# Layer 1's row maxima formed as b + relu(a - b) by three engines, instead of one reduction over 1024 scores

## The reference, cut to what matters

```python
q = q_vec.reshape(B_H, S, QK_DIM)
k = k_vec.reshape(B_H, S, QK_DIM)
qn = jnp.sum(q * q, axis=-1)[:, :, None]
kn = jnp.sum(k * k, axis=-1)[:, None, :]
qk = jnp.einsum('bsd,btd->bst', q, k)
scores = -(qn + kn - 2.0 * qk) / tau
attn = jax.nn.softmax(scores, axis=-1)
out = jnp.einsum('bst,btc->bsc', attn, v)
```

## Time and profile before

| | |
|---|---|
| median of 3 runs | 8861.34 us (8860.65 to 8866.9) |
| span of the profiled execution, first to last instruction | 8833.4 us |
| mean granted TensorE clock in it | 0.889 |
| busy: PE / DVE / ACT / POOL | 84% / 64% / 44% / 25% |
| layers 1 to 3 | from about 3540 us to the end |

### The profile page before, as it was taken

One profiled execution on the slowest core, in us unless ns is written; L12 is line 12 of the kernel. 1 busy time (PEld: TensorE's weight loads), 2 busy tenths in 40 slices (PEclk: granted clock), 3 DMA queues, 4 the chain that ended last, 5 costly groups with the idle time before them and its releaser, 6 DMA issues.

```text
span 8833.4 us, 95654 instructions
## 1 busy us (share of the span) xinstructions
PE 7445.8 (84%) x35246; PEld 3495.5 (40%) x35246; DVE 5679.0 (64%) x9661; ACT 3844.7 (44%) x7430; POOL 2220.5 (25%) x1862
## 2 busy tenths in 40 slices
PE   7989889989989995668888888888888888888867
PEld 4544444445544452123333333333333333333343
DVE  4666656566665663457667667766766766766674
ACT  4444444444544552443543543444354354354330
POOL 1222222222222220012421421331231232133152
PEclk9999999999999996679899889899888888888988
DMA  1111111111111112024444544554444454354375
GB/s 64 35 38 37 36 37 38 40 38 44 42 42 38 41 38 72 4 78 118 153 141 107 169 150 112 149 163 116 133 152 129 117 160 144 97 167 146 99 220 145
DMA packets 244211, 849.75 MB, mean 96 GB/s; under 512 B 46413, under 2 KB 49177, under 8 KB 243361
## 3 DMA queue, kind: packets, MB, share of 16 engines
q1 hardware_dynamic: 150272, 388.71, 16.4%
q0 software_dynamic: 92160, 453.06, 16.2%
q10 hardware_dynamic: 1312, 1.87, 0.1%
HBM read 602.10 MB, written 89.68 MB: 78 GB/s over the span
## 4 chain that ended last, share of the span: by engine, by line
PE 39%; DVE 13%; ACT 6%; DMA 3%; issue 3%; SPq 2%; POOL 1%; DVEq 0%; ACTq 0%; POOLq 0%
PE ps L2189 10%; PE ps L2649 4%; PE ps L2434 4%; DVE arena L1901 4%; PE ps L2199 3%; PE ps L2660 2%; PE ps L2630 2%; PE ps L2127 2%; PE ps L2320 2%; SPq L2683 2%; PE ps L2113 2%; DMA arena<-arena 1%; DVE arena L400 1%; DMA arena<-img,arena 1%; PE ps L2152 1%
## 5 line engine op out<-in xcount | busy, mean ns | idle before, releaser
L2467 POOL DMA_INDIRECT arena<-img,arena x1152 | 1369.8, 1189 | 2685.6 <-DMA img<-arena 1859.8
L2364 DVE SCALAR_TENSOR_TENSOR arena<-arena 128x384 f32<-128x384 f32 x1152 | 748.0, 649 | 656.6 <-DMA arena<-img,arena 653.6
L1901 DVE TENSOR_REDUCE arena<-ps 128x2 f32<-128x1024 f32 x768 | 894.3, 1216 | 322.6 <-PE ps L2168 319.6
L2042 ACT ACTIVATE arena<-ps 128x512 f32<-128x512 f32 x1536 | 817.5, 603 | 315.1 <-PE ps L2199 312.4
L2189 PE MATMUL ps<-arena 128*64 128x512 f32 x3072 | 935.7, 711 | 0.0
L982 POOL TENSOR_TENSOR arena<-arena 128x512 f32<-128x512 f32 x384 | 442.1, 1158 | 1942.5 <-DMA arena<-decay 1942.4
L2649 PE MATMUL ps<-arena 128*64 128x512 f32 x3072 | 808.1, 651 | 129.6 <-DMA arena<-arena 73.9
L2434 PEld LDWEIGHTS ps<-arena 128*96 128x96 f32 x4608 | 557.9, 174 | 202.1 <-issue 201.7
L2434 PE MATMUL ps<-arena 128*96 128x128 f32 x4608 | 610.4, 289 | 26.3 <-DVE arena L2353 26.2
L1115 DVE TENSOR_TENSOR arena<-ps,arena 128x512 f32<-128x512 f32 x384 | 265.4, 691 | 492.3 <-issue 270.5
L949 PE MATMUL ps<-arena 128*128 128x512 f32 x1152 | 507.2, 596 | 0.0
(11 more groups left out here) (344 smaller groups left out, 12092.7 us busy)
## 6 DMA issues: line engine op xcount, KB each, us to landing
arena<-arena SPq DMA_DIRECT2D x1024, 144.5 KB, 2.9
arena<-decay SPq DMA_DIRECT2D x384, 256.0 KB, 3.2
img<-arena SPq DMA_DIRECT2D x162, 384.0 KB, 2.6
arena<-img,arena POOLq DMA_INDIRECT x1152, 4.5
arena<-y SPq DMA_DIRECT2D x16, 768.0 KB, 6.4
arena<-x SPq DMA_DIRECT2D x16, 768.0 KB, 6.3
out<-arena SPq DMA_DIRECT2D x16, 768.0 KB
arena<-x SPq DMA_DIRECT2D x16, 512.0 KB, 5.1
```

The lines of the kernel that those rows point to most:

```text
L1901: dve.tensor_reduce(out, self.wides[B.at("max", b, g, n, h) // 2].rearrange("p (a b) -> p a b", a=2), AX.X, AL.max).then_inc(*S.mark("max_ ...
L2042: act.activation(self.p[n % 6], B("score", b, n)[:, :], ACT.Exp).then_inc(*S.mark("p_act", b, n))
L2364: dve.scalar_tensor_tensor(gb[:, 0:384], gb[:, 384:768], pp[:, 1, n:n + 1], gb[:, 0:384], AL.mult, AL.add).then_inc(*S.mark("corner_x", b, n))
L2467: pool.indirect_dma_start(self.g[n % 6], None, img, bass.IndirectOffsetOnAxis(ap=ii[:, n:n + 1], axis=0)).then_inc(*S.landed(f"{self.tag}g ...
```

## The change

For each block of 128 query rows, a holds the scores of the first 512 keys and b those of the last 512. The largest of both is the largest element of b + relu(a - b). TensorE forms a - b in PSUM with two accumulated matmuls (the second one against `kn`, the negated second half of the keys, which VectorE writes once per g) and b with a third. ScalarE takes the relu of a - b from PSUM into an SBUF buffer of 512 columns (`self.p[m % 4]`, one of four). VectorE adds b to it and keeps the running maximum in one instruction, `tensor_tensor_reduce`, that also writes the sum back into the buffer. So a step has six matmuls, two relus and two `tensor_tensor_reduce` of 512 columns, in place of four matmuls and two reductions of 1024. Banks are now taken one by one from all five, in the order diff, diff, max, max for each step. In layer 3, ScalarE's gelu moves one step of the second stream earlier, so it now stands ahead of the relus of the step that it followed. The joining of the two halves at `mt` becomes a copy.

```diff
@@ Layer1.__init__
+        self.kn = ar([96, 2, 512], BF16)
@@ Layer1.dve, rows
+            if side:
+                dve.wait_ge(*S("split_dve", b, 1, g, 1))
+                dve.tensor_scalar(self.kn[:, g, :], ks[:, g, H(1)], -1.0, None, AL.mult).then_inc(*S.mark("less_k", b, g))
@@ Layer1.dve, maxima
             for n in range(12):
-                for h in range(2):
-                    dve.wait_ge(*S("max_pe", b, g, n, h))
-                    out = mx[:, 24 * h + 2 * n:24 * h + 2 * n + 2]
-                    dve.tensor_reduce(out, self.wides[B.at("max", b, g, n, h) // 2].rearrange("p (a b) -> p a b", a=2), AX.X, AL.max).then_inc(*S.mark("max_dve", b, g, n, h))
+                for m in range(24 * g + 2 * n, 24 * g + 2 * n + 2):
+                    rb = self.p[m % 4]
+                    dve.wait_ge(*S("rise_act", b, m))
+                    dve.wait_ge(*S("max_pe", b, m))
+                    dve.tensor_tensor_reduce(rb, B("max", b, m)[:, :], rb, 1.0, -3.0e38, AL.add, AL.max, mx[:, m:m + 1]).then_inc(*S.mark("max_dve", b, m))
                 yield
...
-                m0, m1 = (bc(mx[:, 24 * h + j:24 * h + 24:3], 3) for h in range(2))
-                i = dve.tensor_tensor(self.mt[:, :, 32 * j + 27:32 * j + 30], m0, m1, AL.max)
+                i = dve.tensor_copy(self.mt[:, :, 32 * j + 27:32 * j + 30], bc(mx[:, 24 * g + j:24 * g + 24:3], 3))
@@ Layer1.act, maxima
-            yield from skip(12)
+            for n in range(12):
+                for m in range(24 * g + 2 * n, 24 * g + 2 * n + 2):
+                    act.wait_ge(*S("diff_pe", b, m))
+                    act.wait_ge(*S("max_dve", b, m - 4))
+                    act.activation(self.p[m % 4], B("diff", b, m)[:, :], ACT.Relu).then_inc(*S.mark("rise_act", b, m))
+                yield
@@ Layer1.pe, maxima
+            pe.wait_ge(*S("less_k", b, g))
             for n in range(12):
-                for h in range(2):
-                    i, free, free2 = B.pair(("max", b, g, n, h), ("max_dve", b, g, n, h))
-                    pe.wait_ge(*free)
-                    pe.wait_ge(*free2)
-                    for q in range(2):
-                        sb, j = divmod(2 * n + q, 3)
-                        r = slice(32 * j, 32 * j + 32)
-                        t = pe.matmul(B.t[i + q][:, :], qs[r, g, 128 * sb:128 * sb + 128], ks[r, g, H(h)], start=True, stop=True)
-                    t.then_inc(*S.mark("max_pe", b, g, n, h))
+                two = []
+                for u in range(2 * n, 2 * n + 2):
+                    sb, j = divmod(u, 3)
+                    two.append((24 * g + u, slice(32 * j, 32 * j + 32), slice(128 * sb, 128 * sb + 128)))
+                diff = []
+                for m, r, q in two:
+                    ps, free = B.take(("diff", b, m), ("rise_act", b, m))
+                    pe.wait_ge(*free)
+                    diff.append(ps)
+                    pe.matmul(ps[:, :], qs[r, g, q], ks[r, g, H(0)], start=True, stop=False)
+                for (m, r, q), ps in zip(two, diff):
+                    pe.matmul(ps[:, :], qs[r, g, q], self.kn[r, g, :], start=False, stop=True).then_inc(*S.mark("diff_pe", b, m))
+                for m, r, q in two:
+                    ps, free = B.take(("max", b, m), ("max_dve", b, m))
+                    pe.wait_ge(*free)
+                    pe.matmul(ps[:, :], qs[r, g, q], ks[r, g, H(1)], start=True, stop=True).then_inc(*S.mark("max_pe", b, m))
                 yield
@@ Layer3.act
-            yield
             if u % 4 == 2:
                 J = u // 4
                 act.table(ACT.Gelu)
...
+            yield
```

More of the change, by code:

```diff
@@ L92, in __init__ @@
             self.tensor_reduce = self.tensor_tensor_scan = self.reciprocal = self.memset = blank
-            self.bn_stats = self.bn_aggr = blank
+            self.bn_stats = self.bn_aggr = self.tensor_tensor_reduce = blank
         else:
@@ L97, in __init__ @@
             self.tensor_tensor_scan, self.reciprocal, self.memset = eng.tensor_tensor_scan, eng.reciprocal, eng.memset
-            self.bn_stats, self.bn_aggr = eng.bn_stats, eng.bn_aggr
+            self.bn_stats, self.bn_aggr, self.tensor_tensor_reduce = eng.bn_stats, eng.bn_aggr, eng.tensor_tensor_reduce
 class Scalar(Engine):
@@ L1897, in maxima @@
             for n in range(12):
-                for h in range(2):
-                    dve.wait_ge(*S("max_pe", b, g, n, h))
-                    out = mx[:, 24 * h + 2 * n:24 * h + 2 * n + 2]
-                    dve.tensor_reduce(out, self.wides[B.at("max", b, g, n, h) // 2].rearrange("p (a b) -> p a b", a=2), AX.X, AL.max).then_inc(*S.mark("max_dve", b, g, n, h))
+                for m in range(24 * g + 2 * n, 24 * g + 2 * n + 2):
[3 more added lines that the diff above has]
+                    dve.tensor_tensor_reduce(rb, B("max", b, m)[:, :], rb, 1.0, -3.0e38, AL.add, AL.max, mx[:, m:m + 1]).then_inc(*S.mark("max_dve", b, m))
                 yield
-            dve.wait_ge(*S("max_dve", b, g, 11, 1))
+            dve.wait_ge(*S("max_dve", b, 24 * g + 23))
             dve.wait_ge(*S("mt_pe", b - 1 + g, 1 - g, 1))
             for j in range(3):
-                m0, m1 = (bc(mx[:, 24 * h + j:24 * h + 24:3], 3) for h in range(2))
-                i = dve.tensor_tensor(self.mt[:, :, 32 * j + 27:32 * j + 30], m0, m1, AL.max)
+                i = dve.tensor_copy(self.mt[:, :, 32 * j + 27:32 * j + 30], bc(mx[:, 24 * g + j:24 * g + 24:3], 3))
             i.then_inc(*S.mark("mt_dve", b, g))
```

## The result

| kernel | median us (lowest to highest) | runs |
|---|---|---|
| before | 8864.01 (8860.65 to 8866.9) | 4 |
| changed | 8943.52 (8933.38 to 8969.57) | 4 |

The changed kernel is slower: ratio 1.0096, 95% interval 1.0079 to 1.0112. The forecast was 8903, so the sign is right, but the loss is about twice the +42 us forecast, and the median lies 1.5 us beyond the upper end of the range. The profiled execution of the changed kernel took 8933.38 us, with a span of 8931.5, 98.1 us longer than the span of before (mean clock 0.888 against 0.889).

The account below looks back on a forecast made before the run. VectorE's reduction was taken to bound images 0 and 1, TensorE image 5. Per image 4.7 - 3.0 + 3.1 = +4.8 us, +67 over 14 images, with -25 for images 0 and 1: +42 on 8861.3, 8903 us; range 8846 to 8942.

Parts of the forecast that it names:

- The failed step: the gelu: Layer 3's gelu, one step earlier, stands ahead of relus and ends no listed wait; no cost was put for it.
- The pads and the relus: Images 2 to 15, g = 1: step 59's relus queue behind the pads on ScalarE, delaying the offset convolution; +3.1 us an image.
- The removed waits: Images 2 to 15: TensorE's waits for VectorE's reductions go, less one new wait of 1.1 us; net -3.0 us an image.
- The third pass: TensorE's extra matmul pair per step in images 2 to 15; 20 passes outside the shadow, +4.7 us an image.
- Images 0 and 1: Maxima with no second stream beside them get faster; -27 us, with the negation -25, between -32 and +5.
- the negation: VectorE writing `kn`, exposed in images 0 and 1: four times some 0.4 us, +2 us; hidden in the other images.
- VectorE's instruction: One `tensor_tensor_reduce` of 512 columns takes 0.75 us, put between 693 and 1216 ns; 0.7 to 0.85 expected in the profile.
- The clock is lost: Rival: TensorE stays at clock 0.50 for longer after the 7 us standstill; 2 us an image, 8930 us, chance 0.12.
- No change: Rival: TensorE's own work takes in the relus' delay behind the pads; +0.8 us an image, 8847 us, chance 0.15.
- The clock comes back: Rival: g = 1's granted clock rises from 0.90 towards full; up to 5 us an image, 8833 us, chance 0.12.
- The instruction at 1216 ns: Rival: VectorE's new instruction is slow, so images 0 and 1 give nothing; +86 us, 8947 us, chance 0.07.
- the passes that don't overlap: Rival: the two accumulating matmuls on TensorE don't run side by side; +57 us, 8960 us, chance 0.04.

Follow-up runs that it names:

- e1: The changed kernel with layer 3's gelu one further step of the second stream earlier, ahead of the relus; 8810.47 us, ratio 0.9946.
- e3: The changed kernel with both moves, the gelu one further step earlier and the two pads one step later; 8740.81 us, ratio 0.9876.
- e2: The changed kernel with the two pads of layer 2's head one step later in ScalarE's order; 8899.97 us, ratio 1.0064.
- e7: The kernel before, old reductions kept, with the gelu two steps earlier, at e1's place; 8795.39 us, ratio 0.994.
- e5: The kernel before with only the change's gelu move, one step of the second stream earlier; 8851.75 us, ratio 0.9996.
- e8: The changed kernel with one diff pass against a bf16-rounded key difference, in place of two accumulated passes; 8928.55 us, ratio 1.009.
- e6: e3 with one diff pass against a bf16-rounded key difference, in place of two accumulated passes; 8746.99 us, ratio 0.9875.
- e4: The kernel before with the new form of the maxima in images 0 and 1 only, old gelu place; 8844.67 us, ratio 1.0001.

## Why the prediction was wrong in size

**The failed step: the gelu.** The prediction said: "The gelu stands one step earlier; it is ahead of relus that would otherwise wait behind it and ends no wait of rows 11." Rows 11 leave out the line of the window 5059 to 5101 us that has such a wait:

```profile
L2649 PE MATMUL ps<-arena 128*64 128x512 f32 x98 | 24.0, 605 | 2.4 <-ACT arena L2611 2.4
```

The prediction looked at what waits behind the gelu and not at what the gelu comes to wait behind. The gelu follows the relus of the step before it in ScalarE's queue, and these are bound to TensorE's progress; its two halves (1.09 us), in g = 1 with the table load ahead (1.28 us), then run right before they are needed. The cost was taken as zero and shows as a new wait of 2.87 us in g = 1 and one of 1.45 us in g = 0, 58.9 us in all. Moving the gelu away also takes half clock with it, 5.0 us an image in g = 0 (e1) and 1.3 to 2.1 in g = 1 (e3 against e2, e1 against changed). The rows of g = 0:

```profile
5111.86 1.09 ACT L2037 ACTIVATE arena<-ps 128x512 f32<-128x512 f32 x2 [2.87 <-PE ps L2182]
5112.83 1.10 ACT L2627 ACTIVATE arena<-ps 128x512 f32<-128x512 f32 x2
```

```profile
5113.49 1.08 PE L2666 MATMUL ps<-arena 128*64 128x512 f32 x4 [1.45 <-ACT arena L2627]
```

(Changed kernel, image 5, g = 0: ScalarE, then TensorE.) In the table the change's own share of what the gelu's place costs is 5.8 - 4.2 = 1.6 us in g = 0 (e1 less e7) and 2.0 to 2.9 in g = 1 (e3 against e2, e1 against changed): 3.6 to 4.5 us an image, 50 to 63 over 14 images and known to some 1 us an image, which is the size of the gap between +42 forecast and +98 in the profiles (the two mis-sized terms below, some -3 and +2.5 us an image, nearly cancel). The timed loss, 79.5 us between the medians, is smaller than the +98 of one pair of executions. The timed ratios say the same more coarsely: with the gelu two steps earlier the change costs 0.06% (e1 against e7) in place of 0.96%, so that 0.9%, some 80 us give or take 30, hangs on the gelu's place. e5 shows that the move alone isn't the cause, and e1 that another place undoes it; what costs is the relus together with the gelu's place. The changed kernel with the gelu left where it was before was not run; whether its own move helped or harmed stays open.

**The pads and the relus: right.** Forecast 3.1 us an image, 7 us of standstill, the convolution 15 us after step 57. Measured 3.6 (e2), 7.01 and 15.8.

**The removed waits: the shadow was right, the sum too high.** Of 5.8 us in g = 1 the prediction let 3.1 vanish in the DMAs' shadow; e3, in which both new stalls are mended or nearly so, waits 3.88 us for the pads in image 5, so the shadow is real. But e3's g = 0 and g = 1 take 102.4 us together and e7's, with the old reductions and the same gelu, 101.2. With the pass worth 1.5 to 1.8 us, the waits removed were worth 0.3 to 0.6 us net, not 3.0. That difference is worked out from two kernels and not tried alone, and it is known to no better than 1 us. TensorE's idle time says where the gain went. In g = 0 it falls from 2.0 us an image in e7 to 0.7 in e3, where 1.1 less was forecast. In g = 1 it stays, 7.5 and 7.2: the 5.7 us behind VectorE's reductions gave way to 2.7 more for the pads, 1.1 for the relus (forecast for step 66 alone; it is 0.63 at step 60 and 0.47 at step 66), 1.1 for the gelu even at its new place, and 0.6 more at line 2677 (line 2660 before), where 0.3 was to go.

**The third pass: over-priced.** Its duration was right: in image 5 the three passes of step 57 start 0.22 us apart. The term was 4.7 us an image, and e8 and e6 measured 1.5 and 1.8. With the pass removed, half clock in the two stretches grows by 5.0 us (e8) and 4.5 us (e6) an image and TensorE's idle time by 0.6 and 1.2 us; at the 0.4 us that a microsecond at half clock cost in e7 these make some 2.6 us in e8 and 3.0 in e6, for 3.2 and 2.9 us missing. That is an estimate; why the half clock grows is not shown. The error has the other sign, and hid part of the gelu's.

**Images 0 and 1: right, and partly given back.** Forecast -27 in the stretches, +2 for the negation; measured -31.3, and the negation, 0.29 us a time on VectorE where 0.4 was put without a row, moves image 0's first maxima by 0.3 us. The twelve steps of image 0 take 18.5 us on VectorE (from 3551.93 to 3570.48) for 19 forecast. The 9.6 us given back behind them, with 21 us more at half clock, were not in the sum. The handovers, put at 0.05 us each without a row, lie between 0.03 and 0.07 us there: TensorE to ScalarE 0.04, ScalarE to VectorE 0.03, VectorE to TensorE 0.07 at the first steps.

**VectorE's instruction: right.** Taken at 0.75 us; VectorE in order of time, changed kernel, image 0:

```profile
3551.93 0.69 DVE L1906 CUSTOM_DVE_ANT_0 arena<-ps,arena 128x512 f32<-128x512 f32 x1 [0.56 <-ACT arena L2037]
3552.54 0.08 DVE L1906 DVE_READ_ACCUMULATOR2_ANT arena<- 128x1 f32 x1
3552.54 0.69 DVE L1906 CUSTOM_DVE_ANT_0 arena<-ps,arena 128x512 f32<-128x512 f32 x1
3553.15 0.08 DVE L1906 DVE_READ_ACCUMULATOR2_ANT arena<- 128x1 f32 x1
3553.23 0.69 DVE L1906 CUSTOM_DVE_ANT_0 arena<-ps,arena 128x512 f32<-128x512 f32 x1
```

A second row of 0.08 us follows each maximum, and two successive starts lie 0.61 and 0.69 us apart. So the trace shows one `tensor_tensor_reduce` as two rows, and the second costs 0.08 us at most. Over the run's 768 such instructions the first row takes 680 to 696 ns and the second 79 to 85; no run shows the 0.85 us at the upper end of what the prediction expected to see.

**The rivals.** "The clock is lost", priced at 2 us an image, is partly true: in the maxima of images 2 to 14 half clock grows from 14.4 to 18.7 us an image. It is no cause of its own, for e3, which only moves the gelu and the pads, has 8.9. "No change" fails by e2: the relus' delay was not taken in. "The clock comes back" needed above 0.95 in g = 1, and it is 0.89. The instruction at 1216 ns and the passes that don't overlap are excluded by the rows of 0.69 and 0.22 us.

## What to carry to other kernels

Before giving work to an engine because it is idle, write down its queue around the new instructions and ask both ways: for which waits of other streams do the new ones stand in line, and which old instructions, ready early until now, come to stand behind the new ones and their waits. An engine at 44% of the span cost this kernel 7 to 8 us an image in this way, and two moves of a `yield` turned +1.0% into -1.2%, of which 0.6% could be had without the change. Price TensorE's work and waits by the clock of their stretch (in the kernel before a pair of line 2168 takes 0.39 us at 1.00, rows 8, and 0.61 at 0.50, rows 6), and before crediting a change with the gain of a mended stall, mend the same stall in the kernel before.

## What the runs showed of the hardware

- A short wait of TensorE can cost more than its length: the 2.39 us of g = 0, taken away in e7, gave 4.2 us an image, with half clock going from 4.2 to 0, and 2.5 us in the two images that had no half clock there. At step 60 of the changed kernel TensorE comes out of its wait slow: in each of images 2 to 14 the granted clock falls from 1.00 to 0.50 during the wait of 6.9 to 7.9 us, and the first matmul behind it takes 0.60 us where the last one before it took 0.37. In image 5 the clock is 1.00 from 5139.31 to 5140.1 us, ahead of the wait of 7.01 us, and 0.50 from 5147.14 to 5148.5, behind it.
- Less work for TensorE can be worth next to nothing: a pass of some 5 us an image gave 1.5 to 1.8. In g = 1 of e6, 24 matmuls fewer came with half clock up from 8.9 to 13.4 us.
- Outside the maxima, TensorE's idle time is nearly the same in all kernels (428 to 435 us for images 2 to 14), and yet the rest of images 2 to 14 takes 2772 us (e3, 730 of them at half clock), 2781 (before, 744) or 2815 (e4, 843). The last two have the same code there. In 19 runs of the kernel before in one series the time goes from 8822.39 us at a mean clock of 0.890 to 8889.77 at 0.881. What decides where the half clock falls was not tried and stays open, and with it whether e4's 21 us are a gain.
- The accumulator read behind VectorE's `tensor_tensor_reduce` of 128x512 takes 0.08 us behind 0.69 us.
